# Attention block with a rebuilt beginning: queries ahead of keys, casts of the keys on ScalarE

## What is computed

```
q = (LN(x) @ Wq.T + bq), k = (ctx @ Wk.T + bk), v = (ctx @ Wv.T + bv)   # 16 heads of 8
scores = q k.T / sqrt(8) + mask;  out = softmax(scores) v;  x = x + out @ Wo.T + bo
x = x + scan_block(LN(x));  x = x + mlp(LN(x))
```

## Time and profile before

| what | value |
|---|---|
| median of 3 runs | 291.2 us (290.73 to 292.55) |
| the profiled execution | 291.72 us |
| its span, first to last instruction | 289.9 us |
| mean granted TensorE clock | 0.959 of full |
| busy share of the span | PE 91%, DVE 77%, ACT 72%, POOL 35% |
| first scores, unit 0 | 23.52 us from the start |
| first step of the main loop (scores of unit 8) | 35.52 us |

### The profile page before, as it was taken

One profiled execution on the slowest core, in us unless ns is written; L12 is line 12 of the kernel. 1 busy time (PEld: TensorE's weight loads), 2 busy tenths in 40 slices (PEclk: granted clock), 3 DMA queues, 4 the chain that ended last, 5 costly groups with the idle time before them and its releaser, 6 DMA issues.

```text
span 289.9 us, 9826 instructions
## 1 busy us (share of the span) xinstructions
PE 264.6 (91%) x3991; PEld 191.7 (66%) x3991; DVE 223.1 (77%) x407; ACT 210.1 (72%) x441; POOL 101.1 (35%) x225
## 2 busy tenths in 40 slices
PE   8699789999999999999999999999999997841975
PEld 7376457676767676676777777777777664631965
DVE  4776878887878999887888898889889941539871
ACT  3575358888788888888888888888887785298032
POOL 5366765634444333333444454411121120100220
PEclk9999869999999999999999999999999999885699
DMA  6896935887532324242333322222222000000001
GB/s 196 293 312 179 290 94 154 241 210 202 165 115 75 119 66 120 77 137 80 118 108 102 119 66 66 67 80 84 70 84 77 2 3 2 1 0 0 0 2 38
DMA packets 21081, 30.55 MB, mean 105 GB/s; under 512 B 4272, under 2 KB 15052, under 8 KB 20908
## 3 DMA queue, kind: packets, MB, share of 16 engines
q1 hardware_dynamic: 17708, 28.00, 31.9%
q0 software_dynamic: 624, 1.06, 1.4%
q10 hardware_dynamic: 2704, 0.85, 1.2%
HBM read 22.43 MB, written 7.47 MB: 103 GB/s over the span
## 4 chain that ended last, share of the span: by engine, by line
PE 81%; DVE 8%; issue 4%; ACT 3%; DMA 2%; POOL 1%; ACTq 0%; POOLq 0%; DVEq 0%
PE ps L494 24%; PE ps L477 15%; PE ps L458 11%; PE ps L587 5%; PE ps L353 4%; PE ps L505 4%; PE ps L548 4%; PE ps L540 3%; PE ps L369 3%; PE ps L347 2%; PE ps L364 2%; DMA x_sb<-in_x_dram 2%; DVE pmax L1305 2%; PE ps L772 1%; ACT probs L877 1%
## 5 line engine op out<-in xcount | busy, mean ns | idle before, releaser
L1305 DVE TENSOR_REDUCE pmax<-ps 128x2 f32<-128x1024 f32 x128 | 156.1, 1224 | 28.8 <-PE ps L458 28.0
L877 ACT ACTIVATE probs<-ps 128x512 f32<-128x512 f32 x256 | 139.0, 595 | 19.9 <-PE ps L477 17.6
L477 PE MATMUL ps<-q_max,k_rows 59*128 59x128 bf16 x1024 | 82.4, 219 | 0.5 <-ACT probs L877 0.2
L494 PE MATMUL ps<-probs,v_all 128*9 128x128 f32 x2048 | 80.8, 276 | 0.7 <-ACT probs L877 0.7
L458 PE MATMUL ps<-k_rows,q_all 56*128 56x512 bf16 x256 | 78.7, 388 | 2.2 <-DVE pmax L1305 2.0
L477 PEld LDWEIGHTS ps<-q_max,k_rows 59*128 59x128 bf16 x1024 | 55.9, 94 | 5.2 <-ACT probs L877 3.1
L494 PEld LDWEIGHTS ps<-probs,v_all 128*9 128x9 f32 x2048 | 43.4, 90 | 14.9 <-ACT probs L877 1.0
L1114 POOL CAST max_cols<-negmax 128x2 bf16<-128x2 f32 x32 | 6.2, 193 | 119.6 <-DVE negmax L1311 119.6
L458 PEld LDWEIGHTS ps<-k_rows,q_all 56*128 56x128 bf16 x256 | 23.2, 94 | 21.3 <-issue 11.3
L347 PE MATMUL ps<-ones 128*128 128x128 f32 x86 | 15.0, 352 | 11.1 <-ACT k_parts L1003 10.1
L347 PEld LDWEIGHTS ps<-ones 128*128 128x128 f32 x86 | 14.5, 265 | 11.5 <-ACT k_parts L1003 10.5
(11 more groups left out here) (186 smaller groups left out, 330.0 us busy)
## 6 DMA issues: line engine op xcount, KB each, us to landing
k_rows<-k_parts_dram SPq DMA_DIRECT2D x59, 192.0 KB
k_parts_dram<-k_parts SPq DMA_DIRECT2D x16, 384.0 KB, 3.7
ctx_buf<-in_ctx_dram SPq DMA_DIRECT2D x16, 256.0 KB, 6.0
k_rows<-k_parts_dram SPq DMA_DIRECT2D x59, 32.0 KB
mask_sb<-in_mask_1x1xSxS_ff_dram SPq DMA_DIRECT2D x1, 1024.0 KB, 8.7
q_all<-q_rows_dram SPq DMA_DIRECT2D x2, 336.0 KB
k_rows<-k_parts_dram POOLq DMA_DIRECT2D x3, 192.0 KB, 3.8
q_rows_dram<-q_parts SPq DMA_DIRECT2D x2, 288.0 KB, 3.7
```

The lines of the kernel that those rows point to most:

```text
L477: t = pe.matmul(dst, k_rows[rows, i % 4, at:at + P], q_max[rows, i % 2, :], start=not masked, stop=True, skip_group_check=masked)
L494: t = pe.matmul(ps[at:at + HEAD_COLS, 6, 0:P], v_all[:, KT * (i // PAIRS) + 4 * c + j, first + HEAD_COLS * h: first + HEAD_COLS * h + HEAD ...
L877: act.activation(probs[:, u % CHUNKS, h, :], ps[:, 4 + h, :], ACT.Exp).then_inc(probs_ready, 1)
L1305: dve.tensor_reduce(pmax[:, i % 2, :, c], ps[:, bank:bank + 2, :], AX.X, ALU.max).then_inc(pmax_ready, 1)
```

## The change

Seven things are altered, all of them before the main loop has settled.

- ACT's queue issues the identity, then batch 0 of x, Wq, and the two bias rows; x's other batches move to SP's queue. On SP, context chunks 4 and 5 are no longer loaded in the first wave.
- PE turns Wq, the biases and the normalised x before it projects the first chunk of keys, and projects the query right after that chunk. The early chunks' keys have a PSUM bank each (4 to 7), so PE no longer waits for r1 between them; their values go to banks 0, 1, 6 and 7.
- The second part of an early key chunk is cast by ACT (`second_k`), the third part subtracted by DVE (`third_k`). The query's parts for batch 0 are made by POOL (`split_q_first_tokens`).
- SP issues the query's stores, x's rest, and then the stores of the keys with context chunks 4 and 5 and the query's load between them, all ahead of the loads of rows; chunks 6 and 7 lie between the two halves of the first head's load.
- DVE fills `k_rows` in three pieces around the work on x; POOL fills the ones of `v_all` after the first root.
- PE sums the mask before it projects chunk 4, not after it has turned chunk 5.
- In `attend`, scores(0) and scores(1) go first, and the projections of chunks 5 to 7 are spread further behind; the last copy of values (`take_vall(7, 7)`) follows the first exponentials, and DVE normalises x's batches 1 to 3 after its second maximum.

```diff
@@ SP
-            for n in range(EARLY, CTX_SLOTS):
-                load_ctx(n)
...
-            store_chunk(0)
-            for n in range(CTX_SLOTS, FIRST):
-                load_ctx(n)
-            for n in range(1, EARLY):
-                store_chunk(n)
-            sp.wait_ge(once("k_ones_ready"), 1)
-            for half in range(2):
+            def load_first_head(half):
                 for c in range(2 * half, 2 * half + 2):
                     sp.wait_ge(k_first[c], 16)
                 load_half_pair(sp, 0, 0, slice(KEYS // 2 * half, KEYS // 2 * half + KEYS // 2), first_heads[half])
+            for part in range(PARTS):
+                if part < 2:
+                    sp.wait_ge(once("q_step"), 2 * part + 2)
+                else:
+                    sp.wait_ge(once("q_parts_ready"), 1)
+                store_q(sp, part, first_tokens)
+            sp.dma_start(x_sb[:, 1:B, :], x[1:B].rearrange("b t d -> t b d")).then_inc(ld["x_rest"], 16)
+            store_chunk(0)
+            load_ctx(EARLY)
+            store_chunk(1)
+            load_ctx(EARLY + 1)
+            sp.wait_ge(once("q_stored"), 16 * 3)
+            sp.wait_ge(once("q_all_zeroed"), 1)
+            load_q(sp, first_tokens, once("q_loaded"))
+            store_chunk(2)
+            store_chunk(3)
+            sp.wait_ge(once("k_ones_ready"), 4)
+            load_first_head(0)
+            for n in range(CTX_SLOTS, FIRST):
+                load_ctx(n)
+            load_first_head(1)
@@ PE, new order
+            turn(ps[:, 2, 0:P], w_kv[:, 0, :]).then_inc(once("kqv_turned"), 1)
+            turn_ctx(1, 1)
+            pe.wait_ge(ld["vec_qk"], 32)
+            pe.transpose(ps[:, 3, 3 * P:3 * P + 2], vec_nat[0:2, :], ident[0:2, 0:2])
+            pe.wait_ge(ld["wq"], 16)
+            turn(ps[:, 3, P:2 * P], w_kv[:, 2, :]).then_inc(once("kqv_turned"), 1)
+            pe.wait_ge(once("xn_ready"), 1)
+            pe.wait_ge(once("kT_ready"), 1)
+            turn_xn(2, 0, 1)
+            pe.wait_ge(once("kT_ready"), 2)
+            project_k(4, 0)
+            pe.wait_ge(once("qT_ready"), 2)
+            pe.matmul(ps[:, 3, 0:P], kvT[:, 2, :], xnT[:, 0:T], start=True, stop=True).then_inc(once("q_done"), 1)
+            turn_ctx(0, 2)
+            project_k(5, 1)
+            turn_ctx(1, 3)
+            project_k(6, 2)
...
+            turn_ctx(4, 4)
+            pe.wait_ge(once("q_step"), 1)
+            pe.wait_ge(once("ones_ready"), 2)
+            pe.wait_ge(once("mask_abs_ready"), 2)
...
             project_k(5, 4)
             pe.wait_ge(ctxT_ready, 5)
             turn_ctx(4, 5)
@@ PE, attend
+                scores(0, masked)
+                scores(1, masked)
                 early_k(5)
                 early_turn(6)
-                scores(0, masked)
-                scores(1, masked)
                 early_v(5)
+                scores(2, masked)
+                early_k(6)
                 pe.wait_ge(v_ready, 3)
                 pe.wait_ge(once("xn_ready"), B)
                 turn_xn(6, 1, B - 1)
-                early_k(6)
+                scores(3, masked)
                 early_turn(7)
...
                 scores(4, masked)
+                early_k(7)
                 pe.wait_ge(once("out_bank_zeroed"), 1)
                 turn_max(0).then_inc(turned, 1)
                 scores(5, masked)
...
                 keyscores(0, 1, masked)
+                early_v(7)
@@ ACT
+            def second_k(n):
+                act.wait_ge(r1_ready, n + 1)
+                copy(k_parts[:, 1, 512 * n:512 * n + 512], k_r1[:, n % 2, :], k2_ready)
@@ DVE
-                dve.wait_ge(r1_ready, n + 1)
-                dve.tensor_copy(k_parts[:, 1, keys], k_r1[:, n % 2, :]).then_inc(k2_ready, 1)
+            def third_k(n):
+                keys = slice(512 * n, 512 * n + 512)
+                dve.wait_ge(k2_ready, n + 1)
+                dve.tensor_tensor(k_parts[:, 2, keys], k_r1[:, n % 2, :], k_parts[:, 1, keys], ALU.subtract
+                                  ).then_inc(once("k3_early_ready"), 1)
...
+            split_q_first(3, first_tokens, 0)
+            for n in range(EARLY):
+                rest_k(n)
+                if n > 0:
+                    third_k(n - 1)
+            third_k(EARLY - 1)
             dve.wait_ge(ld["ident"], 16)
             dve.tensor_copy(ident_bf[:, :], ident[:, :]).then_inc(once("ident_bf_ready"), 1)
```

More of the change, by code:

```diff
@@ L408, in _ @@
-            project_v(6, 2)
-            pe.wait_ge(v_ready, 2)
-            project_v(7, 3)
-            pe.wait_ge(r1_ready, 4)
+            pe.wait_ge(once("q_step"), 1)
+            pe.wait_ge(once("ones_ready"), 2)
+            pe.wait_ge(once("mask_abs_ready"), 2)
+            for half in range(2):
+                t = pe.matmul(ps[0:1, 2, 0:1], mask_abs[:, half:half + 1], ones[:, 0:1], start=half == 0,
+                              stop=half == 1)
+            t.then_inc(once("mask_summed"), 1)
@@ L414, in _ @@
             turn_ctx(4, 5)
-            pe.wait_ge(once("ones_ready"), 2)
-            pe.wait_ge(once("mask_abs_ready"), 2)
-            for half in range(2):
-                t = pe.matmul(ps[0:1, 0, 0:1], mask_abs[:, half:half + 1], ones[:, 0:1], start=half == 0,
-                              stop=half == 1)
-            t.then_inc(once("mask_summed"), 1)
             pe.wait_ge(v_ready, 4)
@@ L670, in attend @@
                 turn_xn(6, 1, B - 1)
-                early_k(6)
+                scores(3, masked)
                 early_turn(7)
-                scores(2, masked)
-                early_v(6)
-                scores(3, masked)
-                early_k(7)
                 pe.wait_ge(once("qT_ready"), 4)
@@ L1095, in binarise @@
                     gp.tensor_tensor(flat(w_bin, sl), flat(w_bin, sl), nat, ALU.add).then_inc(once("w_bin_ready"), 1)
-            for n in range(EARLY):
-                third(n)
-            gp.wait_ge(once("k_ones_ready"), 1)
+            gp.wait_ge(once("k_ones_ready"), 4)
             for half in range(2):
```

127 lines of the change are left out of this document (62 added, 65 removed).

## The result

| | before | after |
|---|---|---|
| median | 290.6 us (288.19 to 293.51, 20 runs) | 292.85 us (290.67 to 293.89, 20 runs) |
| ratio after to before | | 1.0083, 95% interval 1.006 to 1.0106 |
| profiled execution, span | 291.72, 289.9 | 292.55, 290.7 |
| first scores / first step of the loop | 23.52 / 35.52 | 25.65 / 38.78 |
| span less the loop's first step | 254.4 | 251.9 |

The change costs 0.8% where 0.3% was forecast to be won, and the median lies 0.25 above the top of the range. The last line of the table is what the two profiles say together: the loop starts 3.26 later, and what follows is 2.5 shorter. What differs there is the clock: half from 34 to 41 before, full after; behind 230 us the grant was at half for about 17 us in both.

What follows compares the result with a forecast made beforehand. PE alone was taken to set the loop's pace, so only the loop's start could move: 0.9 earlier, 35.52 to 34.6. 291.72 - 0.9 = 290.8, and 290.3 as median since that execution stood 0.5 above it; range 287.9 to 292.6.

Steps and rivals of the forecast that it cites:

- The part on the keys: Early key chunks: DVE 0.7 lighter, third parts at about 12.0 to 16.3, stores of chunks 1 and 3 about 1 earlier.
- the one on the loads of rows: First head's row loads: first loads issued 0.7 earlier, chunk 1's store landing near 18.2, first scores 1.1 sooner.
- First key projection near 7.5, 1.0 lost: PE's start: projection stands behind Wq, biases and x, at about 7.5 where it was 6.45, losing 1.0.
- the start is late: Rival: x, Wq or biases land late, shifting keys' chain 1 to 1.5; nothing won or 0.5 lost; 291.4, chance 0.18.
- Query's parts at 10.8, SP free for the first store at 12.0: Query split on POOL: parts at 10.8, previously 12.74; SP's earlier issues end about 12.0, first key store level with 11.78.
- The mask: PE waits 1.9: Mask's sum ahead of chunk 4's projection: PE waits 1.9 for DVE's mask; `attend` entered at 21.9, previously 21.79.
- Rows at 22.4, scores(0) waiting for a transfer: Start of `attend`: rows arrive about 22.4, so scores(0) and (1) go then instead of 23.52; 1.1 won.
- Turn behind chunk 7's projection: In `attend`: first maximum's turn waits behind chunk 7's projection (0.86), at 30.5 where it was 31.42; 0.9 won.
- The clock falls again: Ramp's end: granted clock taken to fall to half again as in the profile; forecast 290.3, chance 0.46.
- clock stays up: Rival: better filled last stretch of the ramp keeps the clock full; 0.9 + 1.7 = 2.6 won, 288.6, chance 0.22.
- the new wait lowers the clock early: Rival: PE idle about 17.0 to 18.9 and near 22 drops the clock, 3 lost; about 293.5, chance 0.14.
- the order in `attend` was worth 0.9 us: New `attend` order: turn at 30.5, DVE's four maxima as before, loop at about 34.6 instead of 35.52; 0.9 earlier.

Runs made afterwards that it cites:

- Run 1: Changed kernel with context chunks 4 and 5 loaded in the first wave again, not among the key stores; ratio to the kernel before 1.0003.
- run 13: Changed kernel with chunks 4 and 5 in the first wave and two unused 256 KB loads in their places among the key stores; ratio to before 1.0081.
- run 11: Changed kernel, chunks 4 and 5 in the first wave, first key projection ahead of the query, chunks 6 and 7 behind the first key store; ratio to before 1.0046.
- run 12: Kernel before with only x's batch 0 issued right behind the identity, ahead of the biases; ratio to before 0.9994.
- run 2: Changed kernel with the first key projection ahead of the query again and the bias rows issued ahead of Wq; ratio to before 1.0051.
- Run 4: Changed kernel with the mask's sum behind the turn of chunk 5, as in the kernel before; ratio to before 1.0113.
- run 5: Changed kernel with both repairs: chunks 4 and 5 in the first wave, and the first key projection ahead of the query; ratio to before 0.9985.
- run 9: Changed kernel with both repairs, and the turn of the first maximum ahead of chunk 7's projection; ratio to before 1.0001.
- run 18: Changed kernel, first key projection first, chunks 4 and 5 at about 5.5, chunk 7 behind second-half rows, first maximum's turn ahead of chunk 7's projection; ratio to before 1.0011.
- run 3: Changed kernel with the old order in `attend`, including the old places of the last value copy and the normalisation; ratio to before 1.0119.
- run 0: The changed kernel measured again, unaltered; ratio to the kernel before 1.0100.
- run 14: Kernel before with only chunks 6 and 7 moved from behind the first key store to between the halves of the first head's load; ratio to before 1.0086.
- run 10: Changed kernel with both repairs and the old order in `attend`; ratio to before 1.0033.
- run 8: Kernel before with the change's new `attend` alone; ratio to before 1.0071.
- run 6: Kernel before with chunks 4 and 5 loaded between the key stores, and 6 and 7 between the halves of the first head's loads; ratio to before 1.0154.
- run 15: Kernel before with x's batch 0 right behind the identity and chunks 6 and 7 between the halves of the first head's load; ratio to before 1.0080.
- run 16: Changed kernel with the first key projection ahead of the query and chunks 4 and 5 issued at about 5.5, when Wk's turn is copied; ratio to before 0.9974.
- run 17: Changed kernel, first key projection ahead of the query, chunks 4 and 5 at about 5.5, chunk 7 behind the second half's rows; ratio to before 0.9991.

## Why the prediction was wrong

The failing step is a term that was never put in the sum. The part on the keys and the one on the loads of rows laid out when each store is *issued*, took 3.7 to 4.1 to land it and the rest from before, and named the loads of context chunks 4 to 7 nowhere. Their way in between the key stores and the loads of rows was costed at nothing, without naming what covers it. Run 1 takes chunks 4 and 5 away from the key stores and the loss is gone; run 13 puts two loads there that nobody wants soon and has it back: 0.8%.

The profiles show the loop 4.2 later than forecast, 38.78 for 34.6, and this divides otherwise. The third part of chunk 1 was 1.9 late, 16.0 for 14.1, and with it the issue of the rows, 19.95 for 18.2: the late first projection and what hangs on it. The store between them took 3.85, as forecast. The load of rows took 4.43 where the forecast leaves it 3.3; chunks 6 and 7 are issued behind it, and in run 11, which takes them away, it took 2.48. From the first scores to the loop it took 13.1, forecast 12.2. Chunks 4 and 5 are a half microsecond of all this, so how they come to be worth 0.8% in the median stays open.

Point by point:

- *x* landed at 4.07 (forecast 4.6): right, but run 12 shows that it is worth nothing measurable by itself.
- *First key projection near 7.5, 1.0 lost.* It began at 7.79 and ended at 9.7, where it had ended at 7.7: 2.0 lost, since it also took longer. The term was half its size, and it runs through the chain: the third part of chunk 1 at 16.0, not 14.1, and at 14.5 in run 2, which puts the projection back. Run 2's ratio gives it 0.5%, with overlapping intervals. The same price was in the rival "the start is late", which was set at no more than 0.5 us.
- *Query's parts at 10.8, SP free for the first store at 12.0.* POOL's four steps took 0.29 and 0.43 (forecast 0.3 and 0.4) but ended at 12.25, and the first store was issued at 13.92. Mechanism right, the late start again.
- *ACT's casts and DVE's subtractions:* 0.63 and 0.68, forecast 0.5 to 0.6 and 0.7. Near enough.
- *The mask: PE waits 1.9.* 1.67, and at the place named. Run 4 shows that it was no cost, because the rows came later still.
- *Rows at 22.4, scores(0) waiting for a transfer.* They do wait for a transfer, but until 25.65. This is where the forecast left the trace: first rows issued at 19.95, not near 18.2, and 4.43 on the way. In run 5 they are issued at 18.18, as forecast, and the first scores still come only at 23.32, since the load takes 3.92.
- *Turn behind chunk 7's projection:* DVE waits 1.34 for it, as seen. Runs 9 and 18 show that lifting it wins nothing.
- *The clock falls again.* It did not, behind 34, in this or any profile with the new order; the rival "clock stays up" was right in its mechanism, the projections that now lie in the thin stretch, and gave 1.7 for it. The last column puts it at 1 to 2.5 us. It is why the profiles show so little of the 3.26. The Trainium skill, page "TensorE: Matmul & The Clock Gate", section "HAM oscillation", names long idle gaps of PE as what makes the clock fall. Run 12's profile has it falling at 35.5 with PE busy for 0.65 of 2.00 in 32 to 34 and for 1.17 in 34 to 36, and no wait longer than 0.83. The measurement decides, as it did in the prediction.
- *The rival "the new wait lowers the clock early", 293.5,* was nearest in time but not what happened: around the mask the grant was 1.00 in both profiles of the changed kernel. Such a fall is real (runs 3 and 4, from 21 and from 25), only not the rule. An earlier one, which no case named, went with the late start: PE waits of 1.18 for chunk 1 and 0.54 for the normalised x, and half the clock from 7.3 to 10.7, under the first projection. In the other four profiles with this fall the waits up to 8 come to 1.4 to 1.7; in run 0, without it, to 0.78. It did not set the result: run 0 has its loss at a full clock.

That the order in `attend` was worth 0.9 us was half wrong. The new list takes 12.6 from the first scores to the loop where the old takes 12.0, and what it gains it gains before them and by the clock. It belongs with late chunks 6 and 7. Each cell is with everything else as before (before, 14, 8) or with both repairs (10, 11, 5):

| | chunks 6, 7 early | late |
|---|---|---|
| old `attend` | 1.0 (before) | 1.0086 (run 14), 1.0033 (run 10) |
| new `attend` | 1.0071 (run 8), 1.0046 (run 11) | 0.9985 (run 5) |

By the medians each order is at its best with its own placing, and 0.3 to 0.9% worse with the other's. Neither set is complete: the new order with 6 and 7 late was not run in the kernel before, nor the old one with them early in the repaired kernel, and the intervals of 10 and 5 overlap. With chunk 6 late the old order waits for it; with 6 and 7 early the new one only waits longer for rows. Why the new order then loses 0.7% in the median, with a loop that starts level in the profile, was not found.

What stays open is how much of each ratio goes by way of the clock. Run 1 had a mean grant of 0.971, the changed kernel and run 13 had 0.963 and 0.964, and time goes with the grant. Executions at equal grant (0.969 to 0.971) can be set side by side, though they are few. In the batch of runs 0 and 1, ten of before average 290.5, run 1's six 290.8, run 0's three 292.3. The changed kernel's eight in its own batch average 291.6. Run 13's three average 292.6, with 289.9 for before's nine of that batch. So with the clock set aside about half of the loss or more remains. By which wait the crowding brings it is not shown.

## What to carry to other kernels

A load that moves in a diff has two costs: its own landing (chunk 6 in runs 6, 14 and 15), and what it does to the stores and loads that it joins (runs 13 and 11). The second is the one that a list of issue times does not show. Before costing an issue time, lay the DMA share out by microseconds and ask what is bound to go through DRAM and back in the next five; wide prefetches fitted well into the stretch before that (run 16). And an instruction order and the placing of the loads that it consumes are best tried together: in the kernel before, either alone was a loss (runs 8 and 14).

A profile is one execution. Runs 1 and 13 are 0.8% apart in the median and alike in the trace, and run 17 is 1.4 sooner than run 16 in the trace and level in the median. A cause found in a trace has to be tried by an edit, and a median that moves does not say that the trace's cause moved it.

## What the runs showed of the hardware

- The load of rows that ended last took 2.48 from the end of its issue with no chunk issued behind it (run 11) and 3.92 to 4.50 with chunks 6 and 7 issued there (after, runs 1, 2, 5 and 13). This is not the whole of it: in run 8, with none issued there either, POOL's half took 3.81.
- Two loads of 256 KB among the key stores put 0.5 to 0.8 between the third part of chunk 1 and the issue of its rows (six profiles against seven), and cost 0.8% (runs 1 and 13).
- Executions of one kernel differ in the mean granted clock, with most near one of a few values (0.953, 0.959, 0.965, 0.970, 0.976), and the time goes with it: in the changed kernel four average 293.3 at 0.953 and eight 291.6 at 0.970 to 0.971. Part of it is the clock behind 230 us, at half for 14, 17 or 20.5 us.
- The place of the clock's fall followed the order of PE's list: seven of seven profiles with the old `attend` have it between 34 and 44, none of thirteen with the new.
- Early matmuls were slow at a full recorded grant: 2.07 for a projection at 8.17 in run 0, with 1.02 for the same at 10.76.
